# Two rings instead of three sets of banks: the side jobs of an attention stage take places in the PSUM rings of the scores

## The chip, the cores and the metric

The kernel runs on one core of one Trainium2 chip. Times are device microseconds (us) of one execution; three runs of the kernel before gave 914.8, 915.35 and 916.04 us, median 915.35 us.

## The reference, cut to what matters

```python
x = x + 0.5 * ffn(layernorm(x))          # mixture of experts, top 2 of 8
x = x + attn(layernorm(x))
x = x + 0.5 * ffn(layernorm(x))

# attn: x is (16, 512, 128), 16 heads of 8
q, k, v = (x @ W + b, split in heads)
scores = einsum('bthd,bshd->bhts', q, k) / sqrt(8) + alibi
scores = where(causal, -inf, scores)
out = einsum('bhts,bshd->bthd', softmax(scores), v) @ Wo + bo
```

Only the attention stage is touched by the change.

## The kernel before, in words

Three stages follow each other: an expert layer, the attention over 16 sequences of 512 tokens, and the expert layer again. The order of work in the attention is written out by hand in `walk` (line 785), and every engine walks through the same list and does its own part of it. The outer loop `all_steps` runs b from -3 to 16; step b computes the maximum scores of sequence b+1, the exponential scores and the weighted values of sequence b, and prepares sequences b+2 and b+3. Each step has two halves (8 heads each, kept as 4 pairs), and each half has 22 places, n = 0 to 21:

- At each place n, TensorE writes one **max unit** (called M0 to M21 here; `take_max_scores`, line 882) into a PSUM bank, and VectorE reduces it to the negated row maximum (`find_max`, line 1119).
- At 18 of the places (0-3, 5-8, 10-13, 15-18, 20, 21) it also writes one **exp unit** (E0 to E17; `take_exp_scores`, line 909), and ScalarE takes the exponential of it into `probs` (line 1017). M and E units use different 64x64 quarters of the array, so a neighbouring M and E unit run side by side.
- At places 4, 9, 14 and 19 it multiplies the exponentials with the values (`weigh_values`, line 951), one of four parts V3, V0, V1, V2, all into one bank `pv_ps`, which ScalarE copies out once per half (line 1027).
- The **side jobs** stand in the table `SIDE_WORK` (line 571). In the first half: project_q after place 2, shift_hi after 4, turn_o1 after 9, project_k after 12, turn_o after 14, output after 17, project_v after 21. In the second half: shift_lo after 4, turn_o0 after 9, turn_h after 14. A job comes after the M and E unit of its place and before the V part. ScalarE reads the result of seven of them; VectorE reads turn_o0, turn_o1 (a reciprocal and a product, lines 1161 and 1163) and output (line 1153).

The eight PSUM banks are: three for M units (`max_ps`), three for E units (`exp_ps`), one for `pv_ps`, and one, `side_ps`, for all side jobs. Each engine takes its instructions in order, so an instruction that waits holds all behind it on that engine. TensorE's waits for a free bank are:

```python
if m >= RING:                                   # RING = 3, m counts within one sequence
    pe.wait_ge(max_read, b * NM + (m - RING + 1))
elif after(b, 0):
    last = max(k for k in range(NM) if k % RING == m % RING)
    pe.wait_ge(max_read, (b - 1) * NM + (last + 1))
```

A sequence has NM = 44 M units, and its first unit takes bank 0 again. The last unit of the sequence before that used bank 0 is number 42, that is M20 of the second half. The E units have the same rule with 36 units, which three divides. A side job waits for the reader of the side job before it (`pe.wait_ge(side_read, n - 1)`, line 959).

Of the kernel before, what the change touches and what calls it, by code (L numbers as in the profile page):

```python
# [580 lines left out]

MAX_UNITS = 22
# [85 lines left out]
def attention(nc, x, consts, ops):  # L668
# [12 lines left out]
    with ExitStack() as ctx:  # L681
# [58 lines left out]
        turned = sem("turned")  # L740
        side_read = sem("side_read")
        rden_done = sem("rden_done")
        NM, NE, NV = HALVES * MAX_UNITS, HALVES * EXP_UNITS, HALVES * NPV


        order = [what for g in SIDE_WORK for what in g.values()]

        def present(b, what):

            if not isinstance(b, int):  # L750
                return True
# [5 lines left out]
        L = len(order)  # L757
        before = {-3: 0}
        for n in range(-2, NSEQ + 2):
            before[n] = before[n - 1] + sum(present(n - 1, what) for what in order)  # L760

        def use(b, what):

            here = order[:order.index(what) + 1]
            if isinstance(b, int):
                return before[b] + sum(present(b, w) for w in here)
            return b * L + (before[2] - 2 * L + len(here))

# [13 lines left out]
        def there(b):  # L782
            return not isinstance(b, int) or 0 <= b < NSEQ
# [22 lines left out]

        def dve_splits(b, which):
# [3 lines left out]
        def split(eng, ops_of, passed, b, par, half, what):  # L811

            s, n = int(what[-2] == "k"), int(what[-1])
            if n == 0:
                eng.wait_ge(side_read, use(b - 2, "project_k" if s else "project_q"))
# [18 lines left out]
        def _(sp):  # L834
# [8 lines left out]
            def stack(b, par, half, hf):  # L843

                pairs = slice(hf * PAIRS // 2, (hf + 1) * PAIRS // 2)
                if after(b, 1):
                    sp.wait_ge(exp_out, (b - 2) * NE + (hf + 1) * NE // 2)
# [9 lines left out]
            def place_shift(b, par, half, hf):  # L857

                sp.wait_ge(side_read, use(b if hf else b - 1, "shift_hi" if hf else "shift_lo"))
# [21 lines left out]
        def _(pe):  # L881
            def take_max_scores(b, par, half, hf, n):

                i, heads = max_unit(n)
                m = hf * MAX_UNITS + n
# [3 lines left out]
                if m >= RING:  # L889
                    pe.wait_ge(max_read, b * NM + (m - RING + 1))  # L890
                elif after(b, 0):
                    last = max(k for k in range(NM) if k % RING == m % RING)
                    pe.wait_ge(max_read, (b - 1) * NM + (last + 1))
                before_block = i * BLOCK
                width = before_block + BLOCK
                for c, hh in enumerate(heads):
                    r, at = HP * hf + hh, c * width
                    if i > 0:
                        for low in (0, SIDE):
                            nc.tensor.matmul(max_ps[m % RING][low:low + BLOCK, at:at + before_block],  # L900
                                             q_st[par][low:low + FAR_ROW, r, before_block:width],
                                             k_st[par][low:low + FAR_ROW, r, 0:before_block], start=True, stop=True)
                    for low in (0, SIDE):
                        mm = nc.tensor.matmul(max_ps[m % RING][low:low + BLOCK, at + before_block:at + width],  # L904
# [4 lines left out]
            def take_exp_scores(b, par, half, hf, n):  # L909

                m = hf * EXP_UNITS + n
# [3 lines left out]
                if m >= RING:  # L915
                    pe.wait_ge(exp_done, b * NE + (m - RING + 1))
                elif after(b, 0):
                    last = max(k for k in range(NE) if k % RING == m % RING)
                    pe.wait_ge(exp_done, (b - 1) * NE + (last + 1))
                bank = exp_ps[m % RING]  # L920
# [19 lines left out]
            def weigh_values(b, par, hf, k):  # L940

                pe.wait_ge(exp_done, b * NE + (hf * EXP_UNITS + PV_UNITS[k][1]))
                if k == 0:
                    if hf > 0 or after(b, 0):
                        pe.wait_ge(pv_read, b * HALVES + hf)
                    if hf == 0:
                        pe.wait_ge(side_read, use(b - 1, "project_v"))
# [261 lines left out]
```

## Time and profile before

| what | us |
|---|---|
| median of three runs | 915.35 |
| the profiled execution | 917.0 |
| its span, first to last instruction | 915.2 |
| attention, from the first M unit to the last output | 192.3 to 755 |
| TensorE busy | 810.6 (89%) |
| VectorE busy | 700.6 (77%) |
| ScalarE busy | 614.7 (67%) |

The busy time of TensorE is made of matmul records that lie over each other, so it says little of how much of the time is lost in waits. What is used instead are rows of the timeline (start, duration, engine, line, what is written from what, count, and in brackets the idle time of that engine before it with what ended it). PE is the matmul side of TensorE and PEld its weight loads, which is where its waits begin to show.

### The profile page before, as it was taken

To read this page: it belongs to the slowest core of one execution; us is meant where nothing else is said; L and a number is where in the kernel's file an instruction comes from. 1 tells how busy PE (TensorE), PEld (TensorE's weight loads), DVE (VectorE), ACT (ScalarE), POOL (GpSimd) and SP (SyncE) were. 2 spreads that over 40 slices of the span, in tenths; PEclk is the share of its full clock that TensorE was granted. 3 is DMA by queue.
4 is the path that set the end of the run, shared out by engine and by line. 5 is a ranking of instruction groups with operands and counts; after the bars stand their busy time and mean duration, and the time that the engine had idled before them with its cause. 6 is when DMAs were issued, how large, how long until landed. Compare 5 with 4: busy or idle time off the path is not lost. (4 is left out here: it accounts for less than half of the span.)

```text
span 915.2 us, 30391 instructions
## 1 busy us (share of the span) xinstructions
PE 810.6 (89%) x11106; PEld 459.3 (50%) x11106; DVE 700.6 (77%) x2518; ACT 614.7 (67%) x1506; POOL 383.3 (42%) x582
## 2 busy tenths in 40 slices
PE   4999999268999999999999999999999976999997
PEld 2454554024555555555555555555556544545453
DVE  4999998348778777777777877877878414999996
ACT  3777776113777777777777777777777753777775
POOL 3788888322331231241242142143130002788787
PEclk9999999556999999999999999999999996999999
DMA  6600000232332232232242242132131001010111
GB/s 168 109 0 0 0 0 1 71 115 94 107 117 94 75 123 89 74 128 86 72 136 85 66 140 89 62 135 96 60 130 38 3 1 23 25 34 23 34 29 41
DMA packets 59091, 63.50 MB, mean 69 GB/s; under 512 B 8736, under 2 KB 52640, under 8 KB 58848
## 3 DMA queue, kind: packets, MB, share of 16 engines
q1 hardware_dynamic: 58976, 61.88, 21.2%
q8 instruction: 83, 1.36, 0.7%
q14 instruction: 32, 0.26, 0.1%
HBM read 32.24 MB, written 29.36 MB: 67 GB/s over the span
## 5 line engine op out<-in xcount | busy, mean ns | idle before, releaser
L1119 DVE TENSOR_REDUCE att_neg_max<-att_max 128x1 bf16<-128x512 f32 (+6 forms) x704 | 375.3, 589 | 119.8 <-PE att_max L904 116.7
L1017 ACT ACTIVATE att_probs<-att_exp 128x512 f32<-128x512 f32 x576 | 305.1, 600 | 99.6 <-PE att_exp L935 99.4
L900 PE MATMUL att_max<-att_k_st,att_q_st 51*64 51x448 bf16 (+6 forms) x1792 | 193.1, 287 | 25.0 <-DVE att_neg_max L1119 15.8
L926 PE MATMUL att_exp<-att_q_st,att_k_st 53*64 53x512 bf16 (+7 forms) x2048 | 196.3, 289 | 5.0 <-ACT att_probs L1017 4.4
L365 ACT ACTIVATE moe_scaled<-moe_hi,moe_gates 128x128 f32<-128x128 f32 x512 | 145.5, 369 | 68.1 <-PE moe_hi L312 65.0
L525 DVE SCALAR_TENSOR_TENSOR x<-moe_lo,moe_gates,x 128x128 f32 (+1 forms) x512 | 160.1, 338 | 14.2 <-PE moe_lo L306 13.3
L900 PEld LDWEIGHTS att_max<-att_k_st,att_q_st 51*64 51x64 bf16 x1792 | 93.9, 108 | 133.1 <-DVE att_neg_max L1119 89.2
L951 PE MATMUL att_pv<-att_probs,att_v 128*32 128x512 f32 (+7 forms) x2048 | 151.1, 411 | 0.9 <-ACT att_probs L1017 0.9
L904 PE MATMUL att_max<-att_k_st,att_q_st 64*64 64x64 bf16 x2048 | 148.6, 194 | 0.0
L820 POOL TENSOR_SCALAR att_parts<-att_qk 128x512 bf16<-128x512 f32 x31 | 19.1, 617 | 280.0 <-ACT att_qk L1050 280.0
L306 PE MATMUL moe_lo<-moe_we,moe_hT 128*128 128x512 f32 x256 | 136.2, 614 | 0.0
L312 PE MATMUL moe_hi<-moe_we,moe_hT 128*128 128x512 f32 x256 | 133.2, 602 | 0.0
L935 PE MATMUL att_exp<-bf_consts 64*64 64x128 bf16 (+1 forms) x1152 | 125.0, 212 | 0.0
L402 POOL TENSOR_TENSOR moe_part<-moe_scaled 128x256 f32<-128x256 f32 x128 | 93.9, 734 | 38.0 <-ACT moe_scaled L365 31.0
L904 PEld LDWEIGHTS att_max<-att_k_st,att_q_st 64*64 64x64 bf16 x2048 | 99.6, 110 | 0.0
L926 PEld LDWEIGHTS att_exp<-att_q_st,att_k_st 53*64 53x64 bf16 x2048 | 84.1, 106 | 17.4 <-ACT att_probs L1017 14.2
L951 PEld LDWEIGHTS att_pv<-att_probs,att_v 128*32 128x32 f32 x2048 | 55.3, 109 | 51.7 <-issue 33.1
L312 PEld LDWEIGHTS moe_hi<-moe_we,moe_hT 128*128 128x128 f32 x256 | 49.5, 193 | 62.9 <-issue 59.3
L395 POOL TENSOR_TENSOR moe_rstd<-moe_veps,f_consts 128x4 f32<-128x4 f32 x32 | 32.5, 1016 | 110.9 <-DVE moe_veps L454 108.1
L935 PEld LDWEIGHTS att_exp<-bf_consts 64*64 64x64 bf16 x1152 | 64.1, 106 | 10.2
L343 ACT ACTIVATE moe_hn<-x,moe_nmr,moe_rstd 128x128 f32 (+1 forms) x128 | 52.7, 493 | 16.6 <-DVE moe_nmr L459 16.5
L416 POOL TENSOR_TENSOR x<-x,moe_part 128x128 f32 (+1 forms) x128 | 58.5, 457 | 12.7 <-DVE x L525 12.5
(82 smaller groups left out, 955.9 us busy)
## 6 DMA issues: line engine op xcount, KB each, us to landing
qk_parts<-att_parts SPq DMA_DIRECT2D x32, 384.0 KB, 3.3
att_q_st<-qk_parts SPq DMA_DIRECT2D x64, 192.0 KB
att_k_st<-qk_parts SPq DMA_DIRECT2D x64, 192.0 KB
qk_parts<-att_parts SPq DMA_DIRECT2D x32, 256.0 KB, 2.8
x<-in_L_attn_x SPq DMA_DIRECT2D x16, 256.0 KB, 3.0
qk_parts<-att_parts SPq DMA_DIRECT2D x32, 128.0 KB, 3.4
out<-x SPq DMA_DIRECT2D x16, 256.0 KB, 2.3
moe_we<-in_L_ffn_We SPq DMA_DIRECT2D x2, 512.0 KB, 4.7
```

Of the source, the lines that this page charges most:

```text
L306: nc.tensor.matmul(lo_ps[t][:], hT[par][:, t * P:(t + 1) * P], we[:, 0:HE, :], start=True, stop=True).then_inc(lo_out, 1)
L312: nc.tensor.matmul(hi_ps[t % 2][:], hT[par][:, t * P:(t + 1) * P], we[:, HE:E, :], start=True, stop=True).then_inc(hi_out, 1)
L365: ins = nc.scalar.activation(scaled[t % 2][:, e, :], hi_ps[t % 2][:, e, :], ACT.Copy, scale=gates[par][:, t, HE + e:HE + e + 1])
L402: nc.gpsimd.tensor_tensor(part2[t % 2][:], scaled[t % 2][:, 0:2, :], scaled[t % 2][:, 2:4, :], ALU.add).then_inc(part_step, 1)
L525: nc.vector.scalar_tensor_tensor(out=xt(b, t), in0=lo_ps[t][:, e, :], scalar=gates[par][:, t, e:e + 1], in1=xt(b, t), op0=ALU.mult, op1=AL ...
L900: nc.tensor.matmul(max_ps[m % RING][low:low + BLOCK, at:at + before_block], q_st[par][low:low + FAR_ROW, r, before_block:width], k_st[par] ...
L904: mm = nc.tensor.matmul(max_ps[m % RING][low:low + BLOCK, at + before_block:at + width], q_st[par][low:low + SIDE, r, before_block:width], ...
L926: nc.tensor.matmul(bank[out_at:out_at + BLOCK, c:c + S - j * BLOCK], k_st[par][low:low + FINE_ROW, r, j * BLOCK:(j + 1) * BLOCK], q_st[par ...
L935: mm = nc.tensor.matmul(blocks[:, 0:step_to * len(parts) - step_to + 1:step_to, :], consts.ident_b[low:low + BLOCK, low:low + BLOCK], rows ...
L951: mm = nc.tensor.matmul(pv_ps[VW * hh:VW * (hh + 1), j * BLOCK:S], v[par][:, j, HP * hf + hh, :], probs[:, n, c:c + S - j * BLOCK], start= ...
L1017: nc.scalar.activation(probs[:, n, :], exp_ps[m % RING][:], ACT.Exp).then_inc(exp_done, 1)
L1119: nc.vector.tensor_reduce(neg_max[par][:, hf, heads[0]:heads[0] + len(heads), i], max_ps[m % RING][:, 0:len(heads) * width].rearrange("p ( ...
```

## The change

Side jobs no longer have a bank. Jobs that VectorE reads take the next place in the ring of the M units, which gets a fourth bank; jobs that ScalarE reads take the next place in the ring of the E units, which stays at three. The places are counted through the whole stage in the order of `walk`, so a ring isn't started anew with each sequence. A unit or job waits for the reader of the one that many places before it. Side jobs now signal `max_out`/`exp_out` and their readers `max_read`/`exp_done`. The bias matmul ahead of the steps uses `pv_ps`.

```diff
+DVE_READS = ("turn_o0", "turn_o1", "output")
...
-        RING = 3
-        max_ps = [ps(f"max{i}", [P, S]) for i in range(RING)]
-        exp_ps = [ps(f"exp{i}", [P, S]) for i in range(RING)]
+        MAX_RING, EXP_RING = 4, 3
+        max_ps = ps("max", [P, MAX_RING, S])
+        exp_ps = ps("exp", [P, EXP_RING, S])
         pv_ps = ps("pv", [P, S])
-        side_ps = ps("side", [P, S])
...
+        max_at, exp_at = {}, {}
+        for b in range(-3, NSEQ + 1):
+            walk(b, b % 2, b // 2, lambda c, par, half, hf, n: max_at.update({(c, hf, n): len(max_at)}),
+                 lambda c, par, half, hf, n: exp_at.update({(c, hf, n): len(exp_at)}), None,
+                 lambda c, par, half, what: (max_at if what in DVE_READS else exp_at).update(
+                     {(c, what): len(max_at if what in DVE_READS else exp_at)}))
+        def max_bank(key):
+            return max_ps[:, max_at[key] % MAX_RING, :]
...
+            def wait_max_bank(key):
+                if max_at[key] >= MAX_RING:
+                    pe.wait_ge(max_read, max_at[key] - MAX_RING + 1)
+            def wait_exp_bank(key):
+                if exp_at[key] >= EXP_RING:
+                    pe.wait_ge(exp_done, exp_at[key] - EXP_RING + 1)
...
             def side(b, par, half, what):
-                n = use(b, what)
-                if not isinstance(n, int) or n > 1:
-                    pe.wait_ge(side_read, n - 1)
+                if what in DVE_READS:
+                    wait_max_bank((b, what))
+                    side_ps = max_bank((b, what))
+                else:
+                    wait_exp_bank((b, what))
+                    side_ps = exp_bank((b, what))
...
                 elif what in ("project_q", "project_k"):
+                    pe.wait_ge(exp_done, exp_at[b - 1, "turn_h"] + 1)
...
                 elif what == "project_v":
+                    pe.wait_ge(exp_done, exp_at[b - 2, "turn_h"] + 1)
...
                 elif what == "turn_o":
-                    pe.wait_ge(side_read, use(b, "turn_o1"))
+                    pe.wait_ge(max_read, max_at[b, "turn_o1"] + 1)
...
                 elif what == "output":
+                    pe.wait_ge(exp_done, exp_at[b, "turn_o"] + 1)
...
-                mm.then_inc(turned, 1)
+                mm.then_inc(max_out if what in DVE_READS else exp_out, 1)
```

The waits of the readers and of the queue of the DMAs are rewritten to the same events under their new counts. VectorE gets one wait more before each of turn_o0 and turn_o1, for its own product of the turn before.

## Rows read from the trace of the kernel before

**Rows 1.** The page: busy time, share of the span and instructions of each engine.

```profile
PE 810.6 (89%) x11106; PEld 459.3 (50%) x11106; DVE 700.6 (77%) x2518; ACT 614.7 (67%) x1506; POOL 383.3 (42%) x582
```

**Rows 2.** Windows, first M to first M of next sequence: busy by engine, clock, DMA share.

```profile
192.27:221.91 29.64, 26.83 (x281) 14.09 (x281) 23.53 (x54) 5.07 (x10) 9.32 (x10) 0.56 0.35 122
...
221.91:253.78 31.87, 29.55 (x590) 16.93 (x590) 24.96 (x57) 23.43 (x48) 9.36 (x10) 0.94 0.23 78
...
422.78:456.62 33.84, 31.18 (x630) 18.92 (x631) 26.43 (x60) 25.07 (x51) 9.35 (x10) 1.00 0.29 97
...
691.26:720.51 29.25, 28.44 (x620) 18.05 (x622) 24.45 (x49) 20.96 (x43) 0.00 (x0) 1.00 0.10 31
```

**Rows 3.** What ended idle time before L900's, then L926's instructions: us, times.

```profile
  DVE att_neg_max L1119: 105.0, 221
...
  ACT att_probs L1017: 18.6, 49
```

**Rows 4.** Timeline, TensorE's weight loads, start of step 6.

```profile
422.78 0.14 PEld L900 LDWEIGHTS att_max<-att_k_st,att_q_st 51*64 51x64 bf16 x2 [0.61 <-issue]
...
423.84 0.30 PEld L965 LDWEIGHTS att_side<-att_hT,att_wq 128*128 128x128 f32 x2 [0.23 <-issue]
...
425.75 0.09 PEld L978 LDWEIGHTS att_side<-bf_consts,att_neg_max 128*32 128x32 bf16 x1 [0.49 <-ACT att_qk L1050]
```

**Rows 5.** Timeline, VectorE and ScalarE, start of step 6.

```profile
421.97 0.70 DVE L1119 TENSOR_REDUCE att_neg_max<-att_max 128x4 bf16<-128x512 f32 x1 [0.30 <-PE att_max L904]
...
422.15 1.09 ACT L1017 ACTIVATE att_probs<-att_exp 128x512 f32<-128x512 f32 x2 [0.90 <-PE att_exp L935]
...
423.45 0.60 ACT L1017 ACTIVATE att_probs<-att_exp 128x512 f32<-128x512 f32 x1 [0.22 <-PE att_exp L935]
```

**Rows 6.** Timeline, TensorE's matmuls, places 8 and 9 and turn_o1.

```profile
428.31 0.32 PE L900 MATMUL att_max<-att_k_st,att_q_st 51*64 51x320 bf16 x2
...
428.50 0.41 PE L926 MATMUL att_exp<-att_q_st,att_k_st 53*64 53x448 bf16 x4
...
428.84 0.32 PE L900 MATMUL att_max<-att_k_st,att_q_st 51*64 51x320 bf16 x2
...
429.13 0.33 PE L992 MATMUL att_side<-f_consts,att_oT 128*128 128x128 f32 x1
```

**Rows 7.** Timeline, VectorE (M5, M6) and ScalarE (E4), same places.

```profile
427.63 1.16 DVE L1119 TENSOR_REDUCE att_neg_max<-att_max 128x1 bf16<-128x448 f32 x2 [1.05 <-PE att_max L904]
...
427.85 0.59 ACT L1017 ACTIVATE att_probs<-att_exp 128x512 f32<-128x512 f32 x1
```

**Rows 8.** Timeline, turn_o on TensorE; E8 and project_k's read on ScalarE.

```profile
433.57 0.42 PEld L983 LDWEIGHTS att_side<-f_consts,att_o 128*128 128x128 f32 x4 [0.53 <-ACT att_qk L1050]
...
431.23 0.60 ACT L1017 ACTIVATE att_probs<-att_exp 128x512 f32<-128x512 f32 x1 [1.31 <-PE att_exp L935]
...
432.84 0.69 ACT L1050 ACTIVATE att_qk<-att_side,att_bk_col 128x512 f32<-128x512 f32 x1
```

**Rows 9.** Timeline, second half: E3, M4, shift_lo on TensorE; reads of project_v, E0.

```profile
442.45 0.11 PEld L926 LDWEIGHTS att_exp<-att_q_st,att_k_st 53*64 53x64 bf16 x2 [0.51 <-ACT att_probs L1017]
...
443.17 0.11 PEld L900 LDWEIGHTS att_max<-att_k_st,att_q_st 51*64 51x64 bf16 x2 [0.59 <-DVE att_neg_max L1119]
...
443.48 0.09 PEld L978 LDWEIGHTS att_side<-bf_consts,att_neg_max 128*32 128x32 bf16 x1 [0.17 <-issue]
...
440.72 1.19 ACT L1039 ACTIVATE att_v<-att_side 64x512 f32<-64x512 f32 x2 [0.28 <-PE att_side L971]
...
441.82 0.58 ACT L1017 ACTIVATE att_probs<-att_exp 128x512 f32<-128x512 f32 x1
```

**Rows 10.** Timeline, TensorE's weight loads: E15, the last M19 and V2 of the half.

```profile
453.68 0.14 PEld L926 LDWEIGHTS att_exp<-att_q_st,att_k_st 53*64 53x64 bf16 x4
...
454.03 0.11 PEld L900 LDWEIGHTS att_max<-att_k_st,att_q_st 51*64 51x64 bf16 x2
...
454.32 0.16 PEld L951 LDWEIGHTS att_pv<-att_probs,att_v 128*32 128x32 f32 x8
```

More of the change, by code:

```diff
@@ L739, in attention @@
         pv_read = sem("pv_read")
[L740 to L741 removed]
         rden_done = sem("rden_done")
[L743 to L746 removed]
+        NV = HALVES * NPV
         def present(b, what):
[L750 to L751 removed]
             offset = {"turn_h": 3, "project_q": 2, "project_k": 2, "project_v": 1, "shift_lo": 1, "shift_hi": 0,
@@ L754, in present @@
             return 0 <= b + offset < NSEQ
[L757 to L767, printed above, removed]
         block = ctx.enter_context(nc.Block())
@@ L814, in split @@
             if n == 0:
-                eng.wait_ge(side_read, use(b - 2, "project_k" if s else "project_q"))
+                eng.wait_ge(exp_done, exp_at[b - 2, "project_k" if s else "project_q"] + 1)
                 if after(b, 0):
@@ L857, in place_shift @@
             def place_shift(b, par, half, hf):
-                sp.wait_ge(side_read, use(b if hf else b - 1, "shift_hi" if hf else "shift_lo"))
+                sp.wait_ge(exp_done, exp_at[(b, "shift_hi") if hf else (b - 1, "shift_lo")] + 1)
                 pairs = slice(hf * HP, (hf + 1) * HP)
@@ L881, in _ @@
         def _(pe):
+            def wait_max_bank(key):
[4 more added lines that the diff above has]
+                    pe.wait_ge(exp_done, exp_at[key] - EXP_RING + 1)
             def take_max_scores(b, par, half, hf, n):
                 i, heads = max_unit(n)
-                m = hf * MAX_UNITS + n
+                bank = max_bank((b, hf, n))
                 if n == 0:
                     pe.wait_ge(stack_in[par][hf], half * (STACK_DMAS * DMA) + STACK_DMAS * DMA)
[L889 to L893, printed above, removed]
+                wait_max_bank((b, hf, n))
                 before_block = i * BLOCK
@@ L909, in take_exp_scores @@
             def take_exp_scores(b, par, half, hf, n):
-                m = hf * EXP_UNITS + n
                 if n == 0:
                     pe.wait_ge(shift_in[par][hf], half * (SHIFT_DMAS * DMA) + SHIFT_DMAS * DMA)
[L915 to L920, printed above, removed]
+                wait_exp_bank((b, hf, n))
+                bank = exp_bank((b, hf, n))
                 parts = exp_unit(n)
@@ L1001, in _ @@
             pe.wait_ge(bv_spread, 1)
-            nc.tensor.matmul(side_ps[:, 0:D], bv_cols[:], w["wo"][:], start=True, stop=True).then_inc(bias_out, 1)
+            nc.tensor.matmul(pv_ps[:, 0:D], bv_cols[:], w["wo"][:], start=True, stop=True).then_inc(bias_out, 1)
             pe.wait_ge(bias_ready, 1)
@@ L1023, in copy_values @@
                 if hf == 1:
-                    act.wait_ge(turned, use(b, "turn_o0"))
-                elif after(b, 0):
-                    act.wait_ge(turned, use(b, "turn_o1"))
+                    act.wait_ge(max_out, max_at[b, "turn_o0"] + 1)
+                elif b > 0:
+                    act.wait_ge(max_out, max_at[b, "turn_o1"] + 1)
                 nc.scalar.activation(oT[:], pv_ps[:], ACT.Copy).then_inc(pv_read, 1)
             def side(b, par, half, what):
-                if what in ("output", "turn_o0", "turn_o1"):
+                if what in DVE_READS:
                     return
-                act.wait_ge(turned, use(b, what))
+                act.wait_ge(exp_out, exp_at[b, what] + 1)
+                side_ps = exp_bank((b, what))
                 if what == "project_v":
@@ L1158, in side @@
                     c = b - 1 if hf else b
-                    dve.wait_ge(turned, use(b, what))
-                    heads = side_ps[:].rearrange("p (t h c) -> p t h c", t=T, c=VS)
+                    last = (b, "turn_o1") if hf == 0 else (b - 1, "turn_o0")
+                    if last in max_at:
+                        dve.wait_ge(max_read, max_at[last] + 1)
+                    heads = side_ps.rearrange("p (t h c) -> p t h c", t=T, c=VS)
                     nc.vector.reciprocal(rden[:].unsqueeze(3), heads[:, :, :, HD:HD + 1]).then_inc(rden_done, 1)
```

56 lines of the change are left out of this document (29 added, 27 removed).

## The prediction

> **What bounds the kernel now.** I read the page first. It gives TensorE 89% of the span, VectorE 77% and ScalarE 67% [rows 1]; none is full, and TensorE's share is one of overlapping records. Next the windows by sequence. A full step of the attention, with all side jobs, takes 33.84 us (there are 12 such steps, b = 1 to 12), VectorE busy for 26.43 us of it and ScalarE for 25.07 [rows 2]. So no engine's own work fills a step; the three hand banks to each other and lose time there. The waits name the hand-over: before the weight loads and matmuls of L900, TensorE was idle 105.0 us in 221 places until a VectorE maximum was done; before those of L926 it was 18.6 us in 49 places until an exponential was done [rows 3]. The reader should see a factor of five, but not take 105 us as the prize. Much of that idle time is normal restart, and where a VectorE wait goes, a ScalarE wait often stands close behind. So the third view is the timeline of one step, unit by unit. A unit that a reader holds starts 0.05 us after that reader's end: E4's read ends at 427.85 + 0.59 = 428.44 [rows 7], E7 starts at 428.50 [rows 6].
>
> **The change part by part.** Nothing is computed more or less, so the whole sum is of waits moved. For each held place I ask which wait is latest under the new rules. Times are of step 6.
>
> *Start of the step.* The old ring begins anew, so M0 waits for M20 of the sequence before, read from 421.97 to 422.67 [rows 5]; M0 starts at 422.78, and 0.61 us idle is booked as "issue" [rows 4]. Continued with four banks, M0 waits for M18, long done: up to 0.6 us free. But project_q is now fourth behind E0 in the ring of three (E0, E1, E2, job). ScalarE reads E16 and E17 until 423.24 and E0 from 423.45 to 424.05 [rows 5]. With E0's scores there earlier, its read starts at about 423.14 (reads follow each other 0.1 us inside the recorded durations) and ends at 423.74, so project_q starts at 423.79, against 423.84 [rows 4]: only 0.05 is left of the 0.6. Then shift_hi, held at 425.75 by the read of the single side bank [rows 4], waits for E2 instead and starts 0.3 us after M4, at 425.36. Gain 0.40; I take 0.35.
>
> *Places 5 to 9, both halves.* M8 (428.31) and M9 (428.84) are held by M5 and M6; E7 between them (428.50) by E4 [rows 6, 7]. Four banks free M8 and M9, but not E7. M9 follows E7 by some 0.15 instead of 0.34, then turn_o1 as the sixth of the ring waits for M6, read until 427.63 + 1.16 = 428.79 [rows 7]. Gain 0.17 in the first half. In the second VectorE is behind after the layernorm statistics and turn_o0 is held by M6's read: gain 0.02.
>
> *Places 10 to 14, first half.* project_k comes after E8 is read, at 431.83 [rows 8], that is some 0.20 later than now. turn_o now starts at 433.57, right behind project_k's read, which ends at 432.84 + 0.69 = 433.53 [rows 8]. In the ring it waits for E10, done earlier, and follows M14 by 0.3 us; that frees 0.43. Net 0.23. In the second half turn_h waits for normalised rows from ScalarE in any case: 0.
>
> *Places 0 to 4, second half.* The largest term. project_v's two reads run from 440.72 to 441.91 and E0's until 442.40 [rows 9]. New: E2 waits for project_v, 441.96, which is 0.85 later than now (a loss taken alone). E3 waits for E0 as before, 442.45 [rows 9]; so E2's delay ends inside a wait that was there anyway. M4 was held by M1, which VectorE reads only after 0.86 us of statistics, to 443.17 [rows 9]; with four banks it waits for M0 and follows E3 by 0.2, at 442.65. shift_lo and V3 follow 0.31 later, at 442.96 against 443.48 [rows 9]. Gain 0.52.
>
> *Places 15 to 19, second half.* E15 (453.68) stays held, M19 (454.03) comes 0.2 sooner and V2 (454.32) with it [rows 10]. Gain 0.20.
>
> *Waits added.* project_q, project_k, project_v and output get a second wait on TensorE. No row isolates it. From above: M0, with two waits, starts at 422.78 when its reader ended at 422.67 [rows 4, 5], 0.06 over the usual 0.05; four of these are 0.24 us a step. From below: nothing, where TensorE's queue runs ahead. Behind each stand the M, E and V units on TensorE. I take 0.1, nearer to nothing, since only project_q and project_k wait at all. VectorE's added waits are for its own long finished product: 0.
>
> *What is not moved.* The SP queue issues the same DMAs on the same events. GpSimd waits for the reads of project_q and project_k, and is busy 9.35 us of 33.84 [rows 2].
>
> *Sum.* 0.35 + 0.17 + 0.02 + 0.23 + 0.52 + 0.20 - 0.1 = 1.39, say 1.4 us for a full step, 33.84 to 32.4. Twelve give 16.8. Step 0 lacks three jobs (1.1); step 13 lacks turn_h (1.4); step 14, 29.25 us long, lacks the projections and the statistics, so the largest term is missing (0.8) [rows 2]. Step -1 (29.64 us at a clock of 0.56, M units only) is paced by VectorE; three jobs could start one reduction, some 0.5 us, earlier each: 1.1, allowing for the normalised rows. The last steps lose 0.1. Together 21.1 us. The profiled execution took 917.0 us, 1.65 above the median; the terms are differences and are taken from the median of 915.35: **894 us**. Bounds by the unknown parts: with the added waits at 0.24 and the start at nothing, 0.9 a step and 901; with all second-order help (the next group starts with emptier rings), some 1.8 a step and 889.
>
> *A page against it.* The trace has 123.6 us of named reader waits [rows 3]. The Trainium skill reports of a matmul kernel that double-buffering PSUM gave no further gain (TensorE: Matmul & The Clock Gate, "HAM oscillation — how this bites in real kernels"); by that rule the time would stay at 915. There the waits were for DMA. Here the rows name the PSUM reader, so I follow the rows, and give that outcome a small chance below.
>
> **The rivals.**
>
> *ScalarE takes over (907).* Wherever VectorE's wait goes, an exponential is found due at the same moment. For: in the three largest places an E unit stands between the M units [rows 6, 9, 10]. Against: it is already in the sum at its present time. If the terms behind E3, E7 and E15 vanish, 0.35 + 0.23 - 0.1 = 0.48 is left a step, 8 us in all with the other steps.
>
> *No net change (915).* The gains above sit in different stretches, each ended by V work that waits for nothing, but one more VectorE turn of 0.8 us in the M ring could delay M13 or M10 as much. For: turn_o0 is read 1.2 us after it is written. Against: M13 needs it only four units on.
>
> *Side jobs clog the ring of exponentials (923).* Seven jobs a step take one of three banks, and each then asks that ScalarE be no more than two units behind. Place: project_q, project_k and E2 behind project_v, which show 0.0, 0.2 and 0.85 us already. It decides from an average delay of 0.21 us per job (1.5 / 7) not covered by another wait; at 0.3 it costs 7 x 0.3 - 1.5 = 0.6 us a step, 8 us in all. Against: the worst of them, E2, is fully covered.
>
> *More comes back (884).* Gains could compound, since ScalarE's work also moves forward: 2.2 us a step. For: the spacing of unheld units (0.2 us per M) leaves over 6 us of waits in a step. Against: the chains V3, copy, E4, E7 are ScalarE's own latencies.
>
> **How the numbers follow.** Chances: forecast 0.66 (own range 889 to 901), ScalarE takes over 0.13, no net change 0.05, clogged 0.06, more comes back 0.10. The range takes in the second and the last: 883 to 907. Run-to-run differences of this kernel are about 0.1 to 0.2%, so I count within 0.2% (1.8 us) as no change. Faster: 0.66 + 0.13 + 0.10 = 0.89; the same 0.05; slower 0.06.
>
> **What would show it.** In full steps of the trace after: a length of 32.4 us. M0 some 0.3 us after the last E17 with no idle time booked as issue. project_q held by E0's read and E2 of the second half by project_v's, E3 at its old distance from that read, and M4 0.2 us behind E3. turn_o 0.3 us behind M14. E7 and E15 still held by ScalarE. The idle time before L900 that VectorE ends drops to well under half of 105 us, that before L926 rises above 18.6. The prediction is wrong if E3 is later behind project_v's read than now, if ScalarE's waits grow as much as VectorE's fall, or if the granted clock, 1.00 in full steps [rows 2], falls.

## The result, and the profile after

The changed kernel takes **885.19 us** (median of four executions, 883.68 to 885.71) against 915.35 before, a ratio of 0.967 [0.966, 0.969]. The forecast was 894 with a range of 883 to 907: the direction and the range held, but 30.2 us came back where 21.1 were forecast, and the time lies below the forecast's own range (889 to 901), in the part that the range took in for the rival "more comes back". One execution of an experiment below, max3exp4, was in a slower state (1128.42 us at a granted clock of 0.652) and stands in no ratio. The profiled execution took 885.71 us, its span 883.9, which is 31.3 us less than the 915.2 of before. The ledger below divides these 31.3 us.

The page of the kernel after, busy time of each engine (answers to [rows 1]):

```profile
PE 778.4 (88%) x11106; PEld 434.8 (49%) x11106; DVE 695.0 (79%) x2518; ACT 611.5 (69%) x1506; POOL 383.0 (43%) x582
```

The work is the same to the instruction; TensorE's busy time falls by 32.2 us with the same instructions, so what got shorter are its records, which lie over each other, include waits and are longer at the lower clock; how the fall divides among these was not measured. Its share hardly moves (89% to 88%), so the page alone would not have shown what happened. Next the windows of the kernel after, from the first M unit of one sequence to that of the next (steps -1, 0, 6 and 14; length, busy time of PE, PEld, DVE, ACT and POOL, granted clock, DMA share, GB/s; answers to [rows 2]):

```profile
191.20:217.38 26.18, 23.11 (x281) 12.15 (x282) 22.42 (x52) 5.07 (x10) 9.32 (x10) 0.70 0.35 124
217.38:246.10 28.72, 26.41 (x584) 15.42 (x585) 24.81 (x57) 22.71 (x46) 9.35 (x10) 0.97 0.30 101
406.97:439.14 32.17, 29.51 (x646) 17.45 (x635) 26.07 (x60) 24.84 (x50) 9.35 (x10) 1.00 0.31 102
662.65:691.30 28.65, 26.77 (x642) 16.36 (x632) 25.02 (x51) 21.47 (x44) 0.00 (x0) 1.00 0.10 31
```

| stretch | before | after | gained | forecast |
|---|---|---|---|---|
| up to the first M unit | 192.27 | 191.20 | 1.1 | 0 |
| step -1 | 29.64 | 26.18 | 3.5 | 1.1 |
| step 0 | 31.87 | 28.72 | 3.2 | 1.1 |
| steps 1 to 12 | 405.69 | 386.09 | 19.6 | 16.8 |
| step 13 | 31.79 | 30.46 | 1.3 | 1.4 |
| step 14 | 29.25 | 28.65 | 0.6 | 0.8 |
| step 15 to the last output | 34.33 | 35.44 | -1.1 | -0.1 |
| second expert layer | 160.35 | 157.2 | 3.2 | 0 |
| sum | 915.2 | 883.9 | 31.3 | 21.1 |

Two things stand out. The twelve full steps gave 1.63 us each on the mean where 1.4 were forecast; and 11.7 us came from outside them where 4.3 were forecast, 3.2 of these in a layer that the change does not touch. The stretch from step 15 to the last output lost 1.1 where 0.1 was forecast.

Now the waits of the kernel after, the idle time ahead of L900's instructions and then of L921's, which is L926 of before (us, times; answers to [rows 3]):

```profile
  DVE att_neg_max L1119: 76.4, 146
...
  issue: 2.3, 5
```

```profile
  ACT att_probs L1017: 50.5, 154
  ACT att_v L1040: 19.3, 30
```

VectorE's waits fall from 105.0 us to 76.4 and from 221 to 146; ScalarE's rise from 18.6 to 50.5, and 19.3 us are new behind the read of project_v. Idle time booked as issue ahead of L900, 21.5 us before, is 2.3. In sum 145.1 us became 148.5, and the kernel is 3.3% faster. This is the warning of the case for readers of this view: an idle time is booked on the wait that ended last, the M and E units run side by side, and one wait of 0.4 us that now stands ahead of an E unit stands where a longer one on an M unit stood before.

The first step after in single rows, TensorE's weight loads at the start of step 6 (start, duration; a side job that ScalarE reads is now written into `att_exp`): M0, E1, E2, project_q (L964), shift_hi (L978). They answer to [rows 4].

```profile
406.97 0.11 PEld L900 LDWEIGHTS att_max<-att_k_st,att_q_st 51*64 51x64 bf16 x2
...
407.88 0.10 PEld L921 LDWEIGHTS att_exp<-att_q_st,att_k_st 53*64 53x64 bf16 x2 [0.46 <-ACT att_probs L1017]
...
408.36 0.11 PEld L921 LDWEIGHTS att_exp<-att_q_st,att_k_st 53*64 53x64 bf16 x2 [0.34 <-ACT att_probs L1017]
...
408.85 0.30 PEld L964 LDWEIGHTS att_exp<-att_hT,att_wq 128*128 128x128 f32 x2 [0.35 <-ACT att_probs L1017]
...
410.44 0.09 PEld L978 LDWEIGHTS att_exp<-bf_consts,att_neg_max 128*32 128x32 bf16 x1 [0.17 <-issue]
```

M0 no longer waits for the end of the sequence before, and the 0.61 us booked as issue in [rows 4] are gone. project_q waits for ScalarE, as the prediction's first step said; E1 and E2 wait for it too, which it did not name. Counted from M20 of the sequence before (421.48 before, 406.56 after), project_q starts 2.29 us later instead of 2.36, so 0.07 of the 0.6 us is kept (0.05 forecast). From project_q to shift_hi it is 1.59 us instead of 1.91: these 0.32 come from the release of the single side bank and are most of the gain of 0.39.

TensorE's weight loads of the kernel after in the first half: E7, turn_o1 (L993), V0, project_k (L964), turn_o (L983), answering to [rows 6, 8]:

```profile
413.19 0.10 PEld L921 LDWEIGHTS att_exp<-att_q_st,att_k_st 53*64 53x64 bf16 x2 [0.40 <-ACT att_probs L1017]
...
413.59 0.42 PEld L993 LDWEIGHTS att_max<-f_consts,att_oT 128*128 128x128 f32 x4
414.18 0.16 PEld L946 LDWEIGHTS att_pv<-att_probs,att_v 128*32 128x32 f32 x8 [0.17 <-ACT att_probs L1017]
...
416.34 0.30 PEld L964 LDWEIGHTS att_exp<-att_hT,att_wk 128*128 128x128 f32 x2 [0.30 <-ACT att_probs L1017]
...
417.80 0.42 PEld L983 LDWEIGHTS att_exp<-f_consts,att_o 128*128 128x128 f32 x4
```

M9 and turn_o1 follow E7 without a wait of their own, and turn_o stands 0.40 us behind M14 (417.40) with none.

The second half of the kernel after: E2, E3, M4, shift_lo (L978), turn_o0 (L993), turn_h (L961), E15, V2. They answer to [rows 9, 10].

```profile
426.20 0.11 PEld L921 LDWEIGHTS att_exp<-att_q_st,att_k_st 53*64 53x64 bf16 x2 [0.78 <-ACT att_v L1040]
...
426.68 0.11 PEld L921 LDWEIGHTS att_exp<-att_q_st,att_k_st 53*64 53x64 bf16 x2 [0.33 <-ACT att_probs L1017]
426.69 0.11 PEld L900 LDWEIGHTS att_max<-att_k_st,att_q_st 51*64 51x64 bf16 x2
...
427.16 0.09 PEld L978 LDWEIGHTS att_exp<-bf_consts,att_neg_max 128*32 128x32 bf16 x1 [0.33 <-ACT att_probs L1017]
...
430.52 0.42 PEld L993 LDWEIGHTS att_max<-f_consts,att_oT 128*128 128x128 f32 x4 [0.29 <-DVE att_neg_max L1119]
...
434.58 0.42 PEld L961 LDWEIGHTS att_exp<-f_consts,att_hn 128*128 128x128 f32 x4 [1.01 <-ACT att_probs L1017]
...
437.34 0.11 PEld L921 LDWEIGHTS att_exp<-att_q_st,att_k_st 53*64 53x64 bf16 x2 [0.32 <-ACT att_probs L1017]
...
437.73 0.16 PEld L946 LDWEIGHTS att_pv<-att_probs,att_v 128*32 128x32 f32 x8
```

This is the largest step of the prediction. E2 waits 0.78 us for project_v's read (L1040). E3 follows 0.48 later, and M4 is now 0.01 us behind E3, where it was 0.72 behind in [rows 9] and waited for VectorE. From E3 to shift_lo it is 0.48 us instead of 1.03. One wait there is not in the prediction: shift_lo comes fourth behind E1 in the ring of three and starts 0.05 us after ScalarE has read E1, at 426.53 + 0.58 = 427.11. ScalarE's row of that read:

```profile
426.53 0.58 ACT L1017 ACTIVATE att_probs<-att_exp 128x512 f32<-128x512 f32 x1
```

So M4 came 0.19 us sooner behind E3 than forecast and shift_lo 0.16 later behind M4 (0.47 instead of 0.31); that the two nearly cancel is luck.

turn_h's wait of 1.01 us is booked on `att_probs`, but what ended just before it is the last normalised row, at 434.47 on ScalarE, 0.11 us before turn_h. In the kernel before it is the same, 450.80 and 0.12.

Cut at the starts of M20 and of the V parts, step 6 compares so (us). The first column begins at M20 of the step before:

| stretch up to | V3 | V0 | V1 | V2 | V3 | V0 | V1 | V2 | M20 | sum |
|---|---|---|---|---|---|---|---|---|---|---|
| before | 4.28 | 3.95 | 4.45 | 3.53 | 5.81 | 3.95 | 4.06 | 2.82 | 1.00 | 33.84 |
| after | 3.89 | 3.72 | 4.21 | 3.53 | 5.25 | 3.94 | 4.06 | 2.56 | 1.00 | 32.17 |
| gained | 0.39 | 0.23 | 0.24 | 0 | 0.56 | 0.01 | 0 | 0.26 | 0 | 1.67 |
| forecast | 0.35 | 0.17 | 0.23 | 0 | 0.52 | 0.02 | 0 | 0.20 | 0 | 1.49 |

The forecast row sums to 1.49; with 0.1 taken off for the added waits it was 1.39.

The untouched layer is shorter in the run in which the clock rose sooner in it. First the kernel after, then the one before, second expert layer, up to the rise of the granted clock and beyond it:

```profile
726.74:741.20 14.46, 6.27 (x23) 4.53 (x24) 6.85 (x50) 4.58 (x11) 2.02 (x2) 0.50 0.19 38
741.20:883.90 142.70, 134.89 (x490) 67.72 (x488) 128.36 (x737) 100.93 (x341) 113.97 (x206) 0.99 0.10 30
```

```profile
754.85:775.10 20.25, 12.30 (x36) 7.91 (x37) 8.92 (x64) 5.72 (x15) 4.21 (x5) 0.58 0.12 27
775.10:915.20 140.10, 131.82 (x477) 65.91 (x475) 126.34 (x722) 99.81 (x337) 111.71 (x203) 0.99 0.10 30
```

Up to the rise the granted clock is 0.50 and 0.58, mostly its lower level (1.2 GHz). The stretch at that level is 17.1 us long in both kernels (724.2 to 741.2 after, 758.1 to 775.1 before); only its place differs. Before, it begins 3.2 us into the layer and lies in it whole. After, it begins 2.6 us ahead of the last output of the attention, so that 14.5 us of it lie in the layer and the rise comes 14.5 us into the layer instead of 20.3. Beyond the rise 142.70 us are left against 140.10, since less had been done by then. So a rise 5.8 us sooner goes with a layer 3.2 us shorter.

The other end of the same stretch is in the last part of the attention. The window of its last 2.57 us, and the output's matmuls of the last sequence, first after and then before:

```profile
724.17:726.74 2.57, 1.84 (x8) 1.55 (x8) 0.69 (x1) 0.00 (x0) 0.00 (x0) 0.50 0.00 0
...
724.06 1.95 PE L987 MATMUL att_max<-att_wo,att_o_fm 128*128 128x128 f32 x8 [0.78 <-ACT att_o_fm L1064]
```

```profile
752.96 1.16 PE L986 MATMUL att_side<-att_wo,att_o_fm 128*128 128x128 f32 x8 [0.69 <-ACT att_o_fm L1063]
```

The same eight matmuls take 1.95 us where they took 1.16: 0.8 of the 1.1 us that this stretch lost.

### The profile page after: what moved, and what is told of

Its sections match the earlier page's. It is cut to its first block and busy times, and to the rows that moved or that the text cites. A ratio compares the mean times of both kernels' runs of the same rounds, so it can differ in the third digit from the quotient of the medians.

```text
span 883.9 us, 30485 instructions
## 1 busy us (share of the span) xinstructions
PE 778.4 (88%) x11106; PEld 434.8 (49%) x11106; DVE 695.0 (79%) x2518; ACT 611.5 (69%) x1506; POOL 383.0 (43%) x582
## 3 DMA queue, kind: packets, MB, share of 16 engines
q1 hardware_dynamic: 58976, 61.88, 22.2%
## 5 line engine op out<-in xcount | busy, mean ns | idle before, releaser
L921 PE MATMUL att_exp<-att_q_st,att_k_st 53*64 53x512 bf16 (+7 forms) x2048 | 201.1, 290 | 22.6 <-ACT att_v L1040 7.6
L900 PE MATMUL att_max<-att_k_st,att_q_st 51*64 51x448 bf16 (+6 forms) x1792 | 187.1, 284 | 9.0 <-DMA att_k_st<-qk_parts 6.0
L904 PE MATMUL att_max<-att_k_st,att_q_st 64*64 64x64 bf16 x2048 | 144.8, 193 | 0.2 <-DVE att_neg_max L1119 0.2
L900 PEld LDWEIGHTS att_max<-att_k_st,att_q_st 51*64 51x64 bf16 x1792 | 93.0, 107 | 93.2 <-DVE att_neg_max L1119 74.1
L921 PEld LDWEIGHTS att_exp<-att_q_st,att_k_st 53*64 53x64 bf16 x2048 | 82.9, 106 | 56.0 <-ACT att_probs L1017 43.1
L343 ACT ACTIVATE moe_hn<-x,moe_nmr,moe_rstd 128x128 f32 (+1 forms) x128 | 52.7, 495 | 17.7 <-DVE moe_nmr L459 17.6
```

The costliest lines, as they stand in the source:

```text
L900: nc.tensor.matmul(bank[low:low + BLOCK, at:at + before_block], q_st[par][low:low + FAR_ROW, r, before_block:width], k_st[par][low:low + F ...
L904: mm = nc.tensor.matmul(bank[low:low + BLOCK, at + before_block:at + width], q_st[par][low:low + SIDE, r, before_block:width], k_st[par][l ...
L921: nc.tensor.matmul(bank[out_at:out_at + BLOCK, c:c + S - j * BLOCK], k_st[par][low:low + FINE_ROW, r, j * BLOCK:(j + 1) * BLOCK], q_st[par ...
```

## The experiments

All times are medians, ratios are to the kernel before on the same chip, with their 95% interval. Theories A and B are those that each expectation names. The kernels before took 914.68 us beside max3 to lean, 916.28 beside warm_before to stats14 and 914.82 beside the last four.

### The fourth bank (max3)

```diff
-        MAX_RING, EXP_RING = 4, 3
+        MAX_RING, EXP_RING = 3, 3
```

> The kernel after with three banks for the maximum scores in place of four (one bank of the eight lies idle); side jobs still take places in the rings. Theory A (the fourth bank brings the gain where M4, M8, M9 and M19 are held): only the start of the step (0.39 us) and turn_o (0.24) stay; turn_o0 and turn_o1 wait one VectorE reduction longer than in the kernel before (2 x 0.24 lost). A full step of 33.7 us, 905 to 916 us in all. Theory B (it is the release of side jobs from their one bank that brings the gain): a full step of 32.2 us and about 885 us.

913.4 us, 0.999 [0.997, 1.001]; full step 33.72. Theory A held, in the step and in the time. With everything of the change but the fourth bank, nothing measurable is gained. Same place of the second half as above, TensorE's weight loads of max3: E3, M4, shift_lo:

```profile
438.93 0.11 PEld L921 LDWEIGHTS att_exp<-att_q_st,att_k_st 53*64 53x64 bf16 x2 [0.33 <-ACT att_probs L1017]
...
439.65 0.11 PEld L900 LDWEIGHTS att_max<-att_k_st,att_q_st 51*64 51x64 bf16 x2 [0.58 <-DVE att_neg_max L1119]
...
439.96 0.09 PEld L978 LDWEIGHTS att_exp<-bf_consts,att_neg_max 128*32 128x32 bf16 x1 [0.17 <-ACT att_probs L1017]
```

M4 waits 0.58 us for VectorE again and E3 to shift_lo is 1.03 us, the old distance. The V3 stretch is 5.81, that of before. Two V0 stretches become longer than before (4.20 against 3.95), since turn_o1 and turn_o0 now take one of three places among the M units; the start of the step keeps its gain (3.89), and so does V1's stretch of the first half (4.21), where turn_o no longer waits for project_k's read. The fourth bank is what the change lives on: beside lean, the kernel after in all but three waits and run on the same chip (885.72), it is worth 28 us, 18.5 of them in the twelve full steps.

### The bank on the other ring (max3exp4)

```diff
-        MAX_RING, EXP_RING = 4, 3
+        MAX_RING, EXP_RING = 3, 4
```

> The kernel after with the eighth bank given to the exponential scores (three banks for maximum scores, four for exponential scores). Theory A (VectorE's reads hold the places where M units wait, and ScalarE's only those behind them): project_q and project_k are free (0.8 + 0.43 us gained), M4, M8, M9 and M19 stay held and the turns lose 2 x 0.24; a full step of 33.1 us, 900 to 906 us. Theory B (any ring with the extra bank will do, since both readers are equally late): a full step of 32.2 us and 885 us.

903.07 us, 0.987 [0.983, 0.990]; full step 33.17. Theory A held here too. TensorE's weight loads of max3exp4, M4 and shift_lo of the second half:

```profile
437.19 0.11 PEld L900 LDWEIGHTS att_max<-att_k_st,att_q_st 51*64 51x64 bf16 x2 [1.07 <-DVE att_neg_max L1119]
...
437.50 0.09 PEld L978 LDWEIGHTS att_exp<-bf_consts,att_neg_max 128*32 128x32 bf16 x1 [0.17 <-ACT att_probs L1017]
```

No E unit waits there any more, yet M4 waits 1.07 us for VectorE and the stretch is 5.80. The gains are at the places where ScalarE's wait is last: 3.55 for the start instead of 3.89, 4.01 for V1 instead of 4.21. Given to the exponentials the bank is worth 0.55 us a step; given to the maxima, 1.55 (33.72 to 32.17).

### Numbering that goes on over sequences (cont3, from the kernel before)

```diff
+                m += b * NM
                 if m >= RING:
-                    pe.wait_ge(max_read, b * NM + (m - RING + 1))
-                elif after(b, 0):
-                    last = max(k for k in range(NM) if k % RING == m % RING)
-                    pe.wait_ge(max_read, (b - 1) * NM + (last + 1))
+                    pe.wait_ge(max_read, m - RING + 1)
```

> The kernel before with only the numbering of the max banks carried on from one sequence to the next (three banks, side jobs in their own bank). M0 no longer waits for M20 of the sequence before. Theory A (project_q waits on ScalarE's pace anyway; most of the 0.6 us is covered): E1 and E2 are held by E16 and E17 and the step gains 0.12 to 0.16 us, 33.7 us, 913 us in all. Theory B (the restart is an independent stall of 0.6 us): 33.2 us a step, 906 us.

913.0 us, 0.997 [0.995, 0.999]; full step 33.65, as theory A had it. Step 6 gains 0.20 at the start (4.08 for 4.28) and nothing elsewhere; on the mean of the twelve it is 0.16. TensorE's weight loads of cont3, M1, which waits instead of M0, and project_q (L963):

```profile
421.58 0.11 PEld L898 LDWEIGHTS att_max<-att_k_st,att_q_st 51*64 51x64 bf16 x2 [0.38 <-DVE att_neg_max L1117]
...
422.51 0.30 PEld L963 LDWEIGHTS att_side<-att_hT,att_wq 128*128 128x128 f32 x2 [0.23 <-issue]
```

By itself the ring begun anew costs 0.2 us a step. That is not half of the 0.39 of the kernel after, though. In cont3 project_q starts 2.17 us after M20 of the sequence before and shift_hi 1.90 behind project_q, still held by the side bank. In max3 and in the kernel after it is 2.29 and 1.59: there project_q waits for E0's read, which leaves 0.07 of the numbering's gain, and shift_hi gives 0.32. The two gains do not add up.

### The added waits (lean)

```diff
-                    pe.wait_ge(exp_done, exp_at[b - 1, "turn_h"] + 1)
+                    if exp_at[b, what] - EXP_RING < exp_at[b - 1, "turn_h"]:
+                        pe.wait_ge(exp_done, exp_at[b - 1, "turn_h"] + 1)
```

and the same for project_v.

> The kernel after without TensorE's second waits of project_q, project_k and project_v for turn_h, which the wait for the ring's bank already covers. If added waits cost what the prediction took (0.1 us a step) a full step falls from 32.17 to 32.1 us and the total to 884; if they are free, both stay (32.17 and 885).

885.72 us, 0.968 [0.965, 0.972]. Full step of lean:

```profile
406.81:438.99 32.18, 29.52 (x646) 17.46 (x637) 26.08 (x60) 24.84 (x50) 9.36 (x10) 1.00 0.31 102
```

32.18 against 32.17. The second waits of the three projections cost nothing that can be seen; the prediction had 0.1 us a step for these and output's (which lean keeps), with a bound of 0.24.

### The clock held up on both sides (warm_before, warm_after)

Both kernels get the same matmuls of constants, 320 columns wide, whose results nobody reads:

```diff
+            def busy(bank, count):
+                for _ in range(count):
+                    nc.tensor.matmul(bank[:, 0:2 * P + BLOCK], consts.ident_b, consts.wide_b, start=True, stop=True)
```

4 before and 16 after the bias matmul, 2, 52 and 30 behind three side jobs of steps -3 and -2, one behind each M unit of sequence 0, and 50 about the start of the second expert layer.

> The kernel before with matmuls of constants, 320 columns wide and read by nobody, in TensorE's idle stretches at the start of the attention (also one after each M unit of sequence 0) and of the second expert layer. Theory A (part of the gain over the forecast, about 2 us in steps -1 and 0 and 3 us in the second expert layer, is the TensorE clock, at its lower level for other stretches in the two kernels): with the clock up, steps -1 and 0 fall from 61.5 us to about 57, and the kernel with the same filling after the change is only 24 to 26 us faster than this one. Theory B (the ramp gains by the fourth bank alone): the clock changes little here, and the difference stays 30 us.

> The same filling in the kernel after. Theory A: steps -1 and 0 take 53 to 54 us against 54.9 unfilled, twelve full steps stay at 386.1 us, and the time falls to 880 to 884. Theory B: no stretch but those with the fillers changes, 885 to 888 us.

911.14 us, 0.995 [0.993, 0.997], and 887.34 us, 0.969 [0.966, 0.972]: 23.8 us between the two, where the plain pair has 30.2. Windows of steps -1 and 0, warm_before and then warm_after:

```profile
188.37:216.45 28.08, 27.64 (x325) 13.60 (x326) 24.32 (x54) 5.07 (x10) 9.36 (x10) 1.00 0.38 136
216.45:246.65 30.20, 27.88 (x590) 16.35 (x590) 24.97 (x57) 23.41 (x48) 9.38 (x10) 1.00 0.25 82
```

```profile
190.03:217.40 27.37, 27.36 (x326) 13.61 (x326) 24.02 (x54) 5.07 (x10) 9.33 (x10) 1.00 0.40 140
217.40:245.58 28.18, 25.69 (x585) 14.93 (x586) 24.06 (x56) 22.71 (x46) 9.34 (x10) 1.00 0.28 89
```

With the granted clock at 1.00 the change brings 0.7 us in step -1 and 2.0 in step 0, together 2.7 where the plain pair shows 6.6 and the forecast said 2.2. The second expert layer takes 161.0 and 160.7 us. By this pair 3.9 us of the gain in steps -1 and 0 and 2.9 in the layer are the clock's place in time and no shorter wait. For step -1 that is an upper bound: with the fillers TensorE is busy for 27.36 of its 27.37 us, so they can cover a gain of the rings. In step 0, which has no fillers (585 matmuls against 584), the time at the lower level went from 3.7 to 1.6 us in the plain pair, and its gain there is 1.1 above that with the clock held up, about half of those 2.1 us. A full step is as without the fillers, 33.79 and 32.18. A came near for the difference (24 to 26 expected, 23.8 measured) and missed the times: warm_before was to have about 57 us for steps -1 and 0 and has 58.3; warm_after was to take 880 to 884, and its steps -1 and 0 take 55.6 us against 54.9 without fillers. The fillers are work too, warm_after is 2 us slower than the kernel it was made from, and keeping the clock up this way paid nothing.

### project_v earlier (pv16)

```diff
-    {2: "project_q", 4: "shift_hi", 9: "turn_o1", 12: "project_k", 14: "turn_o", 17: "output", 21: "project_v"},
+    {2: "project_q", 4: "shift_hi", 9: "turn_o1", 12: "project_k", 14: "turn_o", 16: "project_v", 18: "output"},
```

> The kernel after with project_v moved from place 21 to 16 and output from 17 to 18. E2 of the second half no longer waits 0.9 us for project_v's read. Theory A (that wait is covered: the second half up to turn_o0 is paced by VectorE, which is behind after the statistics, so nothing is won): 32.0 to 32.4 us a full step, 883 to 888 us. Theory B (the wait is a loss by itself): 31.5 us a step, 877 us.

893.66 us, 0.976 [0.973, 0.979]; full step 32.54. Both theories missed: A had the step unchanged (32.0 to 32.4), and it grew by 0.37. Of the 8.0 us between the profiled execution and that of the kernel after, the twelve steps are 4.4, and 2.9 lie in the second expert layer, where the clock rose 20.1 us in. TensorE's weight loads of pv16 in the first half, project_v, output, V2:

```profile
422.56 1.01 PEld L971 LDWEIGHTS att_exp<-att_wv,att_hT 128*64 128x64 f32 x32
...
424.35 0.97 PEld L987 LDWEIGHTS att_max<-att_wo,att_o_fm 128*128 128x128 f32 x8
...
425.73 0.16 PEld L946 LDWEIGHTS att_pv<-att_probs,att_v 128*32 128x32 f32 x8
```

project_v's 32 matmuls take TensorE 1.1 us, and now they stand with output's in one stretch: V2's becomes 4.85 (from 3.53), V3's 3.79 (from 5.25). That alone is a gain of 0.14. But V0's of the second half grows from 3.94 to 4.44. VectorE's statistics sit at places 0 to 2, and with M units there no longer spaced out by E2's wait, M7 to M9 and turn_o0 wait for its reductions (0.19 to 0.40 us each). The wait for project_v's read was covering VectorE's; all3 below, with the statistics elsewhere, has 3.72 in that stretch.

### The statistics out of the second half (stats14)

```diff
-NORMALISE = {(1, 0): "statistics", (1, 1): "aggregate", (1, 2): "add_eps", (1, 5): "take_root", (1, 7): "shift_mean",
+NORMALISE = {(0, 14): "statistics", (0, 15): "aggregate", (0, 16): "add_eps", (1, 5): "take_root", (1, 7): "shift_mean",
```

> The kernel after with VectorE's layernorm statistics (1.4 us with the aggregate and the epsilon) moved from places 0 to 2 of the second half to places 14 to 16 of the first, where VectorE is idle behind V1. Theory A (VectorE paces the second half up to turn_o0): turn_o0 is released 0.3 to 0.8 us sooner, 31.4 to 31.9 us a full step, 875 to 881 us. Theory B (ScalarE's reads of project_v and E0 pace that stretch, as in the four places where E units are held): 32.1 us and 885 us.

883.18 us, 0.964 [0.960, 0.968]; full step 31.96, between theory A (31.4 to 31.9) and theory B (32.1). TensorE's weight loads of stats14 in the second half, E7 and turn_o0:

```profile
427.43 0.11 PEld L921 LDWEIGHTS att_exp<-att_q_st,att_k_st 53*64 53x64 bf16 x2 [0.40 <-ACT att_probs L1017]
...
427.82 0.42 PEld L993 LDWEIGHTS att_max<-f_consts,att_oT 128*128 128x128 f32 x4
```

turn_o0 no longer waits for VectorE (0.29 us in the kernel after), and V0's stretch is 3.72, that of the first half; then E7's wait for ScalarE is the last. VectorE did pace turn_o0, as A had it, but the next wait there, ScalarE's, ended only 0.22 us sooner. The twelve steps give 2.6 us; the two profiled executions differ by only 1.1, because the second expert layer took 159.9 us, 2.7 more, with the clock's rise 20.1 us into it, step -1 took 1.0 more, and the stretch ahead of the first M unit, which varies from run to run, took 2.0 less.

### The same kernel again, and turn_h later (after_again, turn17, stats14_turn17, all3)

```diff
-    {4: "shift_lo", 9: "turn_o0", 14: "turn_h"},
+    {4: "shift_lo", 9: "turn_o0", 17: "turn_h"},
```

stats14_turn17 has this edit and that of stats14, all3 also that of pv16.

> The kernel after once more, beside the next three on the same chip. Theory A (the rest of the gain over the forecast is where the clock of TensorE rises in the second expert layer): 885 us with the clock up about 14 us into that layer, and up to 3 us more where it rises 20 us in; the twelve full steps stay at 386.1 us. Theory B (the second layer's 3 us less has another cause in the change): it takes 157 us again wherever the clock rises.

> The kernel after with turn_h moved from place 14 to 17 of the second half. TensorE now waits there up to 1.3 us for rows that ScalarE normalises at places 8 to 11. Theory A (ScalarE is behind in that stretch, so the waits come back at E12 to E15): V1 starts 1.2 us sooner, V2 only 0.4 to 0.8; 31.4 to 31.8 us a full step, 876 to 880 us. Theory B (the wait is TensorE's alone): 30.9 us a step, 869 us.

> Both moves: statistics at places 14 to 16 of the first half and turn_h at 17 of the second. Theory A (the two stretches are paced one after the other and their gains add): 0.2 us a step less than turn17 alone, 31.2 to 31.6 us, 873 to 878 us. Theory B (they share one chain): the same as the better of the two.

> Those two and project_v at place 16, output at 18. With project_v there the second half up to turn_o0 lost 0.5 us to VectorE's statistics, which are now elsewhere. Theory A (project_v's read then costs in the first half what it frees in the second, 1.3 against 1.5 us): 0.0 to 0.3 us a step less than stats14_turn17. Theory B (statistics and project_v now meet in the first half): 0.3 us or more a step longer.

| kernel | us | ratio to before | full step | second layer | clock's rise in it |
|---|---|---|---|---|---|
| after_again | 884.81 | 0.970 [0.966, 0.974] | 32.17 | 157.5 | 14.7 |
| turn17 | 879.69 | 0.961 [0.957, 0.965] | 31.48 | 160.2 | 20.6 |
| stats14_turn17 | 875.06 | 0.957 [0.954, 0.960] | 31.27 | 160.0 | 20.2 |
| all3 | 870.22 | 0.953 [0.950, 0.955] | 31.13 | 158.0 | 16.1 |

Theory A held for the last three. after_again could not decide, since its clock rose where that of the kernel after did; stats14 and turn17 do. They have the change as well, the clock rises 20 us into their second layer, and it takes 160 us as before the change. So the layer's gain hangs on where the clock rises and is no effect of the rings in it.

TensorE's weight loads of turn17 in the second half, V1, the E unit ahead of turn_h, turn_h (L961), V2:

```profile
430.33 0.16 PEld L946 LDWEIGHTS att_pv<-att_probs,att_v 128*32 128x32 f32 x8
...
432.15 0.14 PEld L921 LDWEIGHTS att_exp<-att_q_st,att_k_st 53*64 53x64 bf16 x4 [0.20 <-ACT att_probs L1017]
...
432.64 0.42 PEld L961 LDWEIGHTS att_exp<-f_consts,att_hn 128*128 128x128 f32 x4 [0.21 <-ACT att_probs L1017]
...
433.70 0.16 PEld L946 LDWEIGHTS att_pv<-att_probs,att_v 128*32 128x32 f32 x8
```

In the kernel after turn_h waits 1.01 us for the normalised rows (434.58 above). Three places later it waits 0.21 us, now for an exponential, V1 is started 1.50 us sooner after V0 and V2's stretch is 0.82 longer: 0.69 a step. The statistics' 0.21 add to it (31.48 to 31.27), and with VectorE's cover gone project_v at place 16 gives 0.14 where alone it cost 0.37. Full step of all3:

```profile
397.68:428.81 31.13, 29.69 (x647) 17.45 (x636) 26.25 (x59) 24.59 (x50) 9.31 (x10) 1.00 0.31 105
```

all3 is 14.6 us faster than the kernel after on the same chip, and is the fastest version here.

## Why the prediction came near, and where it missed

**The steps of a full step.** All eight stretches came within 0.06 us of their terms, and in the main in the way that was named: M0 without a wait, project_q behind E0's read, E2 behind project_v's, M4 close behind E3, turn_o close behind M14. The exception is the end of the largest term, where shift_lo turned out to be held by ScalarE's read of E1, and the size came near because M4 was sooner than forecast by as much. max3 and cont3 show that the causes are the ones named and not others that give the same sums: without the fourth bank the V3 and V2 stretches of the second half return to 5.81 and 2.82 as before, while the start and turn_o, which the prediction put down to the side bank, keep their gain; the numbering alone gives 0.2 at the start and nothing else. Following each held place to the wait that is late next, and only then writing down its gain, is what made these terms good.

**The added waits.** The term of -0.1 was mis-sized: lean has it at 0. The small excess of the other terms is the rest: 1.39 became 1.67 in step 6 and 1.63 on the mean, 2.8 us over the twelve.

**The terms outside the full steps.** Here is the failed part: 4.3 us forecast, 11.7 measured. Their ring part was forecast well as far as it can be told apart: with the clock at 1.00 on both sides steps -1 and 0 give 2.7 (2.2 forecast), and steps 13 and 14 of the plain pair give 1.9 (2.2). What was missing are some 6 us, net, by which the clock's lower stretches lay elsewhere (3.9 in steps -1 and 0 and 2.9 in the layer, less 0.8 at the last output), and 1.1 us of the start, which lies between 188.4 and 192.3 us in the runs whatever the kernel. The prediction took every duration at the clock of before, though [rows 2] showed 0.56 in step -1, the mark of a stretch whose length hangs on more than its waits. The layer's 2.9 are shown by stats14 and turn17 as well. The 3.9 rest on the warm pair, and how step -1 divides between clock and rings stays open, since the fillers filled it. In step -1 the kernels with more time at the lower level are the longer ones: 26.2 us of it in the step's 29.64 before, 22.2 in 28.98 in cont3, 17.7 in 27.90 in max3exp4, 15.9 in 26.18 after; but these kernels differ in their rings too. Why the clock falls and rises where it does was not settled. The kernel after repeats its places (clock's rise 14.5, 14.0 and 14.7 us into the second layer in after, lean and after_again), while stats14, with faster steps, has it at 20.1, so it isn't a plain matter of a shorter attention.

**The rivals.** ScalarE takes over (907): its wait did stand at E3, E7 and E15, but, as the sum had it, at its old time. No net change (915): one more bank in a ring of PSUM banks is worth 28 us here, from max3 (913.4) to the kernel after (885.2), so what the page of the Trainium skill cited with this rival reports of its kernel does not carry over to this one. The Trainium skill says elsewhere that consistent bubbles on the engine that should be busy "can mean there isn't enough SBUF/PSUM for the next tile to be allocated" (Perfetto Trace Analysis, "Optimization Strategy"); that is the sentence which fits, and [rows 3] with max3 bear it out. Clogged (923): E2's delay of 0.78 us is there and covered; pv16 shows what happens when such a cover goes. More comes back (884) had the time almost to the microsecond and is wrong all the same: it wanted 2.2 us a step by gains that compound, and the step gave 1.6. That 885.19 lies inside the stated range is luck to this extent: the range reached down to 883 only for that rival, while the forecast's own ended at 889, and the 6 us of the clock, which neither had, brought the time there.

**The signs.** Two of those named were poor. The idle time before L900 did not fall well under half of 105 us, it fell to 76.4; and "if ScalarE's waits grow as much as VectorE's fall" was to mean failure, yet with project_v's read they grew by 51 us against 29 and the kernel is faster. The length of a step and the distances between units were good signs, the sum of named waits was not.

## What to carry to other kernels

When a PSUM ring is enlarged or shared, cut a step at places that wait for nothing and ask in each stretch which reader is late next; give the spare bank to the ring whose reader ends most stretches last (here 1.55 us a step against 0.55), and try it also with that bank taken out. A long wait on one engine can be the cover of another's, so a job moved alone can lose what it gains together with a second move. Where the profile has stretches at the lower clock, price them apart from the waits and keep some us of the range for them on either side.

## What the runs showed of the hardware that was not expected

- The same second expert layer took 157 to 160.5 us, by when the granted clock rose in it: 14.0 us in, 156.9 (lean); 14.7, 157.5 (after_again); 16.1, 158.0 (all3); 20.3, 160.35 (before). That is some 0.5 us for each us. The spread of 3.5 us is more than the twelve steps of stats14 gained (2.6).
- TensorE's granted clock stayed at 1.00 through a full step of 32.17 us in which it waited some twenty times for 0.2 to 1 us (146 + 154 + 30 waits over 16 steps); the stretches at the lower level lie between 161 and 226 us, around the start of the second expert layer (724 to 741 after, 758 to 775 before) and in the last 3 us of the span.
- A second wait ahead of a matmul whose event is long past had no price (32.18 against 32.17 us for a full step).
